# A block-streamed transformer kernel: order of the work ahead of the first cross attention's block loop

## The chip, the cores and the metric

The kernel runs on one NeuronCore of one Trainium2 chip. The metric is the device time of one execution in microseconds (us); the lower the better. The engines are named as in the profile: PE is the matrix engine (PEld its weight loads), DVE the vector engine, ACT the scalar engine, POOL the general one, and SP the engine that here only issues DMAs. Each runs its own instructions in order, and they wait for one another by semaphores.

## The reference, cut to what matters

Six layers act on x (512 tokens of 512 values): two cross attentions to a context of 8192 rows, two self attentions and two mixtures of experts. The change is in the first cross attention (L0x), which alone normalises queries and keys by head:

```python
q = (x @ Wq.T + bq).reshape(b, s1, h, d)          # x is layer-normed; h = 16 heads, d = 32
kv = (y @ Wkv.T + bkv).reshape(b, s2, 2, h, d)
k, v = kv[:, :, 0], kv[:, :, 1]
q = _ln(q, qn_w, qn_b) * scale                    # _ln: (t - mean) * rsqrt(var + 1e-6) * w + b, over d
k = _ln(k, kn_w, kn_b)
attn = jnp.einsum('bihd,bjhd->bhij', q, k)
attn = jnp.where(padding_mask[:, None, None, :], attn, -jnp.inf)
p = jax.nn.softmax(attn, axis=-1)
out = jnp.einsum('bhij,bjhd->bhid', p, v).reshape(b, s1, c) @ Wo.T + bo
```

## The kernel before, in words

The context is cut into blocks of 512 rows. A list of the blocks in which the mask lets anything through is made at run time; with these inputs the first cross attention has four. It makes two passes over them. The first (`row_maxima`) projects each block's keys and values, stores them in DRAM, and takes the maximum of every query's scores. The second (`weighted_values`) reads them back, takes exponentials and sums. The weights are centred by head first, so that a projected query or key has mean zero in every head, and only its variance has to be taken.

Keys and queries lie transposed, in four chunks of 128 features (four heads each). A block's 16 *quads* are the pairs (chunk c, 128 queries q), chunk by chunk. For a quad PE makes four heads' scores in two pairs of PSUM banks (`quad`, L676 for the scores, L687 adds the mask), and DVE takes a maximum over each pair (`maxima`, L1016, two of 1.2 us for a quad). There are three such pairs of banks: PE may start a half only when DVE is through with the half three before it. Behind each quad PE does two products that prepare the next block (`after_quad`, list `beside`): the key projections of block i + 1 in quads 0 to 7 (`project_keys`, L614, two chunks' worth in quads 0 to 3), then this block's value projections (`project_values`, L651). A product of 128 x 128 by 512 columns in fp32 shows as two matmul records. After quad 8 the variances of the next keys are taken (`variances`, L634), ACT makes roots, DVE inverts them after quads 9 and 10 (L980), and after quad 11 PE spreads them over the features (`spread`, L662) and DVE scales the keys (L987); ACT finishes them (`finish_keys`, L819). ACT also reads each projected chunk out of PSUM (`keys`: a square, L807, and the keys, L808), and in the first blocks counts masked entries of another mask for a later layer (`count`, L796) from four 1 MB loads that SP issues (L566). In the last block there are no next keys: quads 0 to 4 have no product behind them, and the value projections follow from quad 5 on.

Ahead of the loop there is a serial part that does the same for block 0's keys and for the queries. On PE: key projections, `variances(0)`, queries of chunks 0 and 1 (`all_queries`, L625), the spread of the keys (L760), `query_variances(0)` (L748), queries of chunks 2 and 3, `query_variances(2)`, and `query_spread` for both halves (L754). A *query half* is two chunks. ACT squares and reads the projected queries (`squared_query`, L836 and L837), takes roots (`query_roots`, L842), and at the end finishes keys and queries (L819, L846). DVE scales the keys (L1081), inverts a half's roots (`invert_query`, L1072), and then scales the four query chunks (`scale_query`, L1076), all after both inversions. PE enters the loop when all four are scaled.

SP's order: when block 0's keys are projected it loads the context of block 1 for the keys (CT, L516), when the queries are projected the context of block 0 for the values (XNT), then it stores each finished key chunk (L528), and then it enters its loop with the four mask loads.

Of the kernel before, what the change touches and what calls it, by code (L numbers as in the profile page):

```python
# [18 lines left out]
DC = D // P  # L19
# [407 lines left out]
def row_maxima(nc, m, L):  # L427
# [4 lines left out]
    dyn, norm = L.fixed is None, L.norm  # L432
# [28 lines left out]
    NK = DC + 1 if norm else DC  # L461
# [7 lines left out]
    def after_quad(k, todo, first=0):  # L469

        k, n = k - first, NS - first
        return todo[k * len(todo) // n:(k + 1) * len(todo) // n] if k >= 0 else []
# [5 lines left out]
        order.insert(SPREAD_AFTER + 1, "spread")  # L478
    NPAIR = 2 * len(order)
    PRE = 2 if norm else 0  # L480
    begun = L.keys_begun
    further = {sem: 16 for sem in values_stored}
    if begun:
# [24 lines left out]
    class Parts:  # L508
# [86 lines left out]
        def tensor(pe):  # L595
# [95 lines left out]
            def scores(i, ahead):  # L691
                for at, k in enumerate(order if ahead else range(NS)):
                    if k == "spread":
                        spread(i + 1, first_pair(i), at)
                        continue
                    quad(i, at, k)
                    if ahead and norm and k == VAR_AFTER:
                        variances(i + 1)
                    for kind, x, d in after_quad(k, beside) if ahead else after_quad(k, beside_last, 5 if dyn else 0):
                        if kind == "k":  # L700
                            project_keys(i + 1 if dyn else 0, x, d)
                        elif kind == "q":
                            project_queries(x, d)
                        else:
                            project_values(i, x, d, i + 2 if ahead else (i + 1 if dyn else 1))
# [6 lines left out]
            def all_queries(c):  # L712
                if norm:
                    pe.wait_ge(centred, 3 * c + 3)
                for d in range(DC):
                    project_queries(c, d)
# [26 lines left out]
            if norm:  # L743

                def query_variances(first):
                    pe.wait_ge(q_read, first + 2)
                    for c in (first, first + 1):
                        last = t.matmul(m.bank[6 + first // 2][rows(c), :], m.head_cols[:, 0:HD], m.SQ[:, c, :], start=True, stop=True)  # L748
                    last.then_inc(q_variance, 1)

                def query_spread(first):
                    pe.wait_ge(q_inverse, first // 2 + 1)
                    for c in (first, first + 1):
                        t.matmul(m.bank[2 + c], m.head_rows[rows(c), :], m.RSTDQ[rows(c), :], start=True, stop=True).then_inc(q_spread, 1)  # L754
# [7 lines left out]
                pe.wait_ge(k_read, NK + B)  # L762
                query_variances(0)
            all_queries(2)
            all_queries(3)
            if norm:
                query_variances(2)
                pe.wait_ge(scores_taken, PRE + B)
                query_spread(0)
                query_spread(2)  # L770
                pe.wait_ge(q_scaled, DC)
            if not begun:
                pe.wait_ge(wv_loaded, 16)
# [2 lines left out]
            def body(i):  # L776
                with pe.If(i + 1 < nb):
                    scores(i, True)
                with pe.If(i + 1 >= nb):
                    scores(i, False)  # L780

            active_loop(pe, nb, body)
# [3 lines left out]
        def scalar(act):  # L786
# [27 lines left out]
            def finish_keys(j, c, free):  # L814
                act.wait_ge(scores_taken, (B if free is None else spread_pair(free)) + c // 2 + 1)
                act.wait_ge(keys_stored[c], j * 16 + B)
                if free is not None:
                    act.wait_ge(scores_ready, chunk_scored(free, c))
                a.activation(m.KF[:, c, :], m.KW[:, c, :], ACT.Identity, bias=m.vec("kn_b")[:, 0:1],  # L819
                             scale=m.vec("kn_w")[:, 0:1]).then_inc(keys_final, 1)  # L820
# [12 lines left out]
            def squared_query(c):  # L833
                act.wait_ge(q_projected, c + 1)
                b = m.vec(L.bq)[:, c:c + 1]
                a.activation(m.SQ[:, c, :], m.bank[c % 2], ACT.Square, bias=b).then_inc(q_root, 1)  # L836
                a.activation(QF[:, c, :], m.bank[c % 2], ACT.Identity, bias=b).then_inc(q_read, 1)  # L837

            def query_roots(first):
                act.wait_ge(q_variance, first // 2 + 1)  # L840
                s = slice(HD * first, HD * (first + 2))
                a.activation(m.RSTDQ[s, :], m.bank[6 + first // 2][s, :], ACT.Sqrt, bias=m.EPS[s, :]).then_inc(q_root, 1)  # L842

            def finish_query(c):
                act.wait_ge(q_scaled, c + 1)
                a.activation(QF[:, c, :], QF[:, c, :], ACT.Identity, bias=m.vec("qn_b")[:, 0:1],  # L846
                             scale=m.vec("qn_w")[:, 0:1]).then_inc(query_ready, 1)
# [10 lines left out]
            if not begun:  # L858
                act.wait_ge(steps_done, 6)
                keys(0, 0)  # L860
                N.root(act)
                for c in range(1, DC - 1):
                    keys(0, c)
                N.copies(act)
                keys(0, DC - 1)
                key_roots(0)
                squared_query(0)
                squared_query(1)
                query_roots(0)
                squared_query(2)  # L870
                squared_query(3)
                query_roots(2)
                finish_keys(0, 0, None)
                finish_query(0)
                finish_keys(0, 1, None)
                finish_query(1)
                finish_keys(0, 2, None)
                finish_keys(0, 3, None)
                finish_query(2)
                finish_query(3)  # L880

            def masked(i):
# [5 lines left out]
            def body(i):  # L888
                if L.row_mask:
                    masked(i)  # L890

                def count_one(u):
                    if counting:
                        with act.If(i < NB // 4):
                            count(first_iterations(nc, i), u)

                with act.If(i + 1 < nb):
                    keys(i + 1, 0)
                    keys(i + 1, 1)
                    count_one(0)  # L900
                    keys(i + 1, 2)
                    count_one(1)
                    keys(i + 1, 3)
                    if norm:
                        key_roots(i + 1)
                    count_one(2)
                    values(i, 0)
                    values(i, 1)
                    if norm:
                        for c in range(DC - 1):  # L910
                            finish_keys(i + 1, c, i)
                    values(i, 2)
                    count_one(3)
                    values(i, 3)
                    if norm:
                        finish_keys(i + 1, DC - 1, i)
                with act.If(i + 1 >= nb):
                    for kb in range(KT_):
                        count_one(kb)
                        values(i, kb)  # L920
# [49 lines left out]
        def vector(dve):  # L970
# [94 lines left out]
            if norm:  # L1065
                for part in range(4):
                    invert(0, part)

                def invert_query(first):
                    dve.wait_ge(q_root, first + 2 + first // 2 + 1)  # L1070
                    s = m.RSTDQ[HD * first:HD * (first + 2), :]
                    v.reciprocal(s, s).then_inc(q_inverse, 1)  # L1072

                def scale_query(c):
                    dve.wait_ge(q_spread, c + 1)
                    v.tensor_tensor(QF[:, c, :], QF[:, c, :], m.bank[2 + c], ALU.mult).then_inc(q_scaled, 1)  # L1076

                for half in range(2):
                    dve.wait_ge(scores_ready, B + half + 1)
                    s = m.KW[:, 2 * half:2 * half + 2, :]  # L1080
                    v.tensor_tensor(s, s, m.pair[1 + half], ALU.mult).then_inc(scores_taken, 1)  # L1081
                invert_query(0)
                invert_query(2)
                for c in range(DC):
                    scale_query(c)
            else:
                dve.wait_ge(steps_done, 2)
                for c in range(DC):
                    dve.wait_ge(q_projected, c + 1)
                    v.scalar_tensor_tensor(QF[:, c, :], m.bank[c % 2], m.vec(L.bq)[:, c:c + 1],  # L1090
                                           m.RAROWS[:, :], ALU.add, ALU.mult).then_inc(q_read, 1)
# [1128 lines left out]
```

## Time and profile before

| | us |
|---|---|
| median of 3 runs | 1766.46 (1765.86 to 1768.48) |
| the profiled execution | 1768.05 |
| its span, first to last instruction | 1766.3 |
| PE busy, DVE busy, ACT busy in it | 1614.9, 1043.2, 510.7 |
| mean granted PE clock, share of full | 0.957 |

The span is what the rows below are cut from; starts are counted from its first instruction. The part ahead of the first cross attention's loop ends at 62.5 us, its four blocks begin at about 62.5, 122, 179 and 237 us, and its second pass begins at about 292 us. Busy shares say how long an engine worked, not whether anyone waited for it: that is read from the idle time before an instruction and from who ended it.

### The profile page before, as it was taken

Reading aid. Unit: us, or ns where it says so; the run is one execution under the profiler, and the core shown is the slowest. Engines: PE = TensorE matmul, PEld = TensorE weight load, DVE = VectorE, ACT = ScalarE, POOL = GpSimd, SP = SyncE. Lnnn points to the kernel's source line nnn. Section 1 sums busy time; section 2 is a strip of 40 time slices with the busy share of each in tenths; the row PEclk is TensorE's granted clock in tenths of the full one; section 3 lists DMA queues with packets and bytes.
Section 4 is the critical chain, followed back from the end, with each engine's and each line's share of the span. In section 5 each row is a group of like instructions: output and inputs, shape, how many; then the busy total and the mean of one; then the engine's idle time right before and its main releaser. Section 6 shows DMA issues by size and latency. Waiting matters only on the chain. (4 is left out here: it accounts for less than half of the span.)

```text
span 1766.3 us, 27736 instructions
## 1 busy us (share of the span) xinstructions
PE 1614.9 (91%) x9395; PEld 738.8 (42%) x9407; DVE 1043.2 (59%) x1683; ACT 510.7 (29%) x771; POOL 101.3 (6%) x82
## 2 busy tenths in 40 slices
PE   6899998999889889999999699998989789989997
PEld 3233333222333376666665233332222134467775
DVE  5677777999745541111112589997979845743223
ACT  2434325777313310000001111113657512200000
POOL 0100001000002010000001200000200000110001
PEclk9899979999989989999999799988999999989999
DMA  4333442211056966666661313220421021229996
GB/s 161 145 136 116 162 160 80 62 49 36 0 139 111 208 245 238 236 230 231 232 229 48 126 61 113 100 85 31 156 61 48 1 83 31 97 84 335 327 324 226
DMA packets 73577, 244.67 MB, mean 139 GB/s; under 512 B 7344, under 2 KB 20544, under 8 KB 53536
## 3 DMA queue, kind: packets, MB, share of 16 engines
q1 hardware_dynamic: 64896, 224.62, 38.6%
q10 hardware_dynamic: 6048, 10.69, 1.6%
q0 software_dynamic: 2560, 8.39, 1.4%
q8 instruction: 47, 0.77, 0.2%
q14 instruction: 26, 0.21, 0.0%
HBM read 218.24 MB, written 35.91 MB: 144 GB/s over the span
## 5 line engine op out<-in xcount | busy, mean ns | idle before, releaser
L1489 ACT ACTIVATE BIG<-banks 128x1024 f32<-128x1024 f32 (+5 forms) x320 | 282.1, 933 | 132.1 <-PE banks L1428 132.1
L1023 DVE CUSTOM_DVE_ANT_0 BIG<-banks,MASK,MX 128x512 bf16<-128x512 f32 (+5 forms) x384 | 229.1, 655 | 64.3 <-issue 36.8
L2010 PEld LDWEIGHTS banks<-KF,BIG 128*128 128x128 f32 x1792 | 226.9, 191 | 14.1 <-issue 14.1
L2010 PE MATMUL banks<-KF,BIG 128*128 128x160 f32 (+1 forms) x1792 | 229.4, 289 | 2.4 <-DVE KF L1737 2.0
L676 PE MATMUL banks<-KF,XN 32*128 32x512 f32 (+4 forms) x1280 | 200.6, 632 | 18.2 <-DVE MX L1023 9.2
L2038 PE MATMUL banks<-BIG,PB 128*128 128x512 f32 x448 | 202.9, 600 | 0.0
L1425 PE MATMUL banks<-XN,KF 32*128 32x512 f32 (+4 forms) x1280 | 173.7, 613 | 25.9 <-issue 6.9
L1539 DVE TENSOR_TENSOR PB<-PB,BIG 128x2048 f32<-128x2048 f32 (+5 forms) x78 | 166.6, 2136 | 25.5 <-ACT BIG L1489 23.9
L1016 DVE TENSOR_REDUCE MXW<-banks 128x2 f32<-128x1024 f32 x128 | 150.3, 1216 | 52.5 <-PE banks L687 51.5
L651 PE MATMUL banks<-WV,XNT 128*128 128x512 f32 x320 | 162.0, 627 | 0.0
L1391 PE MATMUL banks<-BIG,V 128*32 128x512 f32 (+4 forms) x1280 | 158.5, 566 | 3.7 <-ACT BIG L1489 2.8
L2038 PEld LDWEIGHTS banks<-BIG,PB 128*128 128x128 f32 x448 | 81.5, 190 | 113.1 <-issue 112.9
L676 PEld LDWEIGHTS banks<-KF,XN 32*128 32x128 f32 x1280 | 62.1, 192 | 156.8 <-DVE MX L1023 72.9
L614 PE MATMUL banks<-CT,WK 128*128 128x512 f32 x224 | 115.3, 643 | 4.6 <-DVE WK L419 4.6
L1425 PEld LDWEIGHTS banks<-XN,KF 32*128 32x128 f32 x1280 | 51.4, 187 | 141.6 <-ACT BIG L1489 107.5
L1927 ACT ACTIVATE PS<-banks 128x512 f32<-128x512 f32 x20 | 11.9, 597 | 335.3 <-PE banks L2038 300.8
L1806 DVE TENSOR_TENSOR PB<-V,banks 128x640 f32<-128x640 f32 x32 | 26.3, 821 | 118.6 <-ACT V L1913 114.4
L651 PEld LDWEIGHTS banks<-WV,XNT 128*128 128x128 f32 x320 | 54.6, 191 | 92.5 <-issue 82.9
L1539 DVE TENSOR_TENSOR PS<-PS,BIG 128x2048 f32<-128x2048 f32 (+5 forms) x39 | 82.9, 2126 | 5.7 <-ACT BIG L1489 4.3
L826 ACT ACTIVATE V<-banks 128x512 f32<-128x512 f32 x40 | 23.9, 597 | 210.0 <-PE banks L651 210.0
L1801 DVE TENSOR_SCALAR V<-banks 128x512 f32<-128x512 f32 x24 | 16.6, 691 | 114.8 <-PE banks L2010 112.5
L1539 DVE TENSOR_TENSOR BIG<-BIG 128x2048 f32<-128x2048 f32 (+5 forms) x39 | 80.4, 2062 | 3.8 <-ACT BIG L1489 3.1
(284 smaller groups left out, 1411.3 us busy)
## 6 DMA issues: line engine op xcount, KB each, us to landing
BIG<-in_L0f_w SPq DMA_DIRECT2D x64, 1024.0 KB, 4.8
BIG<-in_L1f_w SPq DMA_DIRECT2D x48, 1024.0 KB, 5.6
BIG<-in_mask_q SPq DMA_DIRECT2D x16, 1024.0 KB, 9.6
CT<-in_ctx SPq DMA_DIRECT2D x9, 1024.0 KB, 4.7
XNT<-in_ctx SPq DMA_DIRECT2D x8, 1024.0 KB, 5.8
k_saved<-KF SPq DMA_DIRECT2D x32, 256.0 KB, 2.6
v_saved<-V SPq DMA_DIRECT2D x24, 256.0 KB, 2.4
KF<-k_saved SPq DMA_DIRECT2D x24, 256.0 KB, 3.4
```

The lines of the kernel that those rows point to most:

```text
L614: last = t.matmul(bank, m.WK[:, d, x * P:(x + 1) * P], KSRC[:, d, :], start=d == 0, stop=d == DC - 1)
L651: last = t.matmul(value_bank(kb), VSRC[:, d, kb * P:(kb + 1) * P], m.WV[:, d, :], start=d == 0, stop=d == DC - 1)
L676: last = t.matmul(m.pair[(2 * at + half) % 3][:, e, k0:k1], QF[rows(g), c, q * P:(q + 1) * P], m.KF[rows(g), c, k0:k1], start=True, stop=n ...
L1016: v.tensor_reduce(m.MXW[:, H * q + h:H * q + h + 2], pair, AX.X, ALU.max).then_inc(scores_taken, 1)
L1023: last = v.tensor_tensor_reduce(m.JUNK[:, 2 * half + e, k0:k1], pair[:, e, k0:k1], bias, 1.0, mx, ALU.add, ALU.max, mx)
L1391: last = t.matmul(m.bank[6 + c % 2][rows(g), q0:q1], m.V[:, kt[k], HD * h:HD * h + HD], m.PE_[:, s % NP, g, q0:q1], start=k == 0, stop=k = ...
L1425: t.matmul(out(g), m.KF[rows(g), c, ks], m.QF[rows(g), c, q0:q1], start=not biases, stop=False)
L1489: a.activation(m.PE_[:, s % NP, 2 * half:2 * half + 2, q0:q1], m.pair[(2 * s + half) % 3][:, :, q0:q1], ACT.Exp).then_inc(exp_ready, 1)
L1539: v.tensor_tensor(dst, dst, m.PE_[:, s % NP, :, q0:q1], ALU.add).then_inc(sum_taken, 1)
L1806: v.tensor_tensor(out, ex, hidden[k % 2], ALU.mult).then_inc(hidden_copied, 1)
L2010: last = t.matmul(out, W1[k][:, d, f * P:(f + 1) * P], XE[:, d, :], start=d == 0, stop=d == DC - 1)
L2038: last = t.matmul(YB, HS[:, 4 * k + f, 0:P], W2[k][:, f, :], start=k + f == 0, stop=(k == NF - 1 and f == 3), skip_group_check=True)
```

## The change

The order of work ahead of the loop is rewritten for this one layer. PE spreads the first query half between the products of query chunk 3, and projects the first two key chunks of block 1 there; inside the loop quads 0 to 3 of block 0 no longer do so, which takes a test of the block's number in each of these quads in every block but the last. ACT finishes keys and the first query half between the squares, and reads the early key chunks ahead of the loop. DVE scales two query chunks behind each inversion.

```diff
--- before.py
+++ after.py
@@ -478,6 +478,8 @@
         order.insert(SPREAD_AFTER + 1, "spread")
     NPAIR = 2 * len(order)
     PRE = 2 if norm else 0
+    EARLY = 2 if norm else 0
+    EARLY_KEYS = [("k", x) for x in range(EARLY)]
     begun = L.keys_begun
     further = {sem: 16 for sem in values_stored}
     if begun:
@@ -696,7 +698,13 @@
                     quad(i, at, k)
                     if ahead and norm and k == VAR_AFTER:
                         variances(i + 1)
-                    for kind, x, d in after_quad(k, beside) if ahead else after_quad(k, beside_last, 5 if dyn else 0):
+                    todo = after_quad(k, beside) if ahead else after_quad(k, beside_last, 5 if dyn else 0)
+                    if ahead and todo[-1][:2] in EARLY_KEYS:
+                        with pe.If(i >= 1):
+                            for _, x, d in todo:
+                                project_keys(i + 1, x, d)
+                        continue
+                    for kind, x, d in todo:
                         if kind == "k":
                             project_keys(i + 1 if dyn else 0, x, d)
                         elif kind == "q":
@@ -762,12 +770,26 @@
                 pe.wait_ge(k_read, NK + B)
                 query_variances(0)
             all_queries(2)
-            all_queries(3)
-            if norm:
-                query_variances(2)
+            if not norm:
+                all_queries(3)
+            else:
+                pe.wait_ge(centred, 3 * DC)
+                project_queries(3, 0)
                 pe.wait_ge(scores_taken, PRE + B)
                 query_spread(0)
+                for d in range(1, DC):
+                    project_queries(3, d)
+
+                project_keys(1, 0, 0)
+                query_variances(2)
+                for d in range(1, DC):
+                    project_keys(1, 0, d)
+                pe.wait_ge(q_root, DC + 2)
+                project_keys(1, 1, 0)
+                project_keys(1, 1, 1)
                 query_spread(2)
+                project_keys(1, 1, 2)
+                project_keys(1, 1, 3)
                 pe.wait_ge(q_scaled, DC)
             if not begun:
                 pe.wait_ge(wv_loaded, 16)
@@ -777,6 +799,9 @@
                 with pe.If(i + 1 < nb):
                     scores(i, True)
                 with pe.If(i + 1 >= nb):
+                    if EARLY:
+                        with pe.If(i < 1):
+                            pe.wait_ge(k_read, NK + EARLY + B)
                     scores(i, False)
 
             active_loop(pe, nb, body)
@@ -867,16 +892,18 @@
                 squared_query(0)
                 squared_query(1)
                 query_roots(0)
+                finish_keys(0, 0, None)
+                finish_keys(0, 1, None)
+                finish_keys(0, 2, None)
                 squared_query(2)
+                finish_keys(0, 3, None)
+                finish_query(0)
+                finish_query(1)
                 squared_query(3)
                 query_roots(2)
-                finish_keys(0, 0, None)
-                finish_query(0)
-                finish_keys(0, 1, None)
-                finish_query(1)
-                finish_keys(0, 2, None)
-                finish_keys(0, 3, None)
+                keys(1, 0)
                 finish_query(2)
+                keys(1, 1)
                 finish_query(3)
 
             def masked(i):
@@ -895,8 +922,13 @@
                             count(first_iterations(nc, i), u)
 
                 with act.If(i + 1 < nb):
-                    keys(i + 1, 0)
-                    keys(i + 1, 1)
+                    if EARLY:
+                        with act.If(i >= 1):
+                            keys(i + 1, 0)
+                            keys(i + 1, 1)
+                    else:
+                        keys(i + 1, 0)
+                        keys(i + 1, 1)
                     count_one(0)
                     keys(i + 1, 2)
                     count_one(1)
@@ -1080,9 +1112,11 @@
                     s = m.KW[:, 2 * half:2 * half + 2, :]
                     v.tensor_tensor(s, s, m.pair[1 + half], ALU.mult).then_inc(scores_taken, 1)
                 invert_query(0)
+                scale_query(0)
+                scale_query(1)
                 invert_query(2)
-                for c in range(DC):
-                    scale_query(c)
+                scale_query(2)
+                scale_query(3)
             else:
                 dve.wait_ge(steps_done, 2)
                 for c in range(DC):
```

## Rows read from the trace of the kernel before

**Rows 1.** The page, busy us, share of the span and instructions of each engine:

```profile
PE 1614.9 (91%) x9395; PEld 738.8 (42%) x9407; DVE 1043.2 (59%) x1683; ACT 510.7 (29%) x771; POOL 101.3 (6%) x82
```

**Rows 2.** Timeline of PE, 52 to 63 us: start, us, operation [idle before <-releaser]:

```profile
52.69 1.05 PE L748 MATMUL banks<-BIG,CON 128*32 128x512 f32 x4 [1.36 <-ACT XN L837]
53.67 1.13 PE L754 MATMUL banks<-BIG,CON 32*128 32x512 f32 x4
57.91 2.08 PE L754 MATMUL banks<-BIG,CON 32*128 32x512 f32 x4 [3.11 <-DVE BIG L1072]
62.53 2.09 PE L676 MATMUL banks<-KF,XN 32*128 32x512 f32 x8 [2.55 <-ACT KF L819]
```

**Rows 3.** Timeline of the other engines, 33 to 61 us:

```profile
33.44 0.35 SPq L516 DMA_DIRECT2D CT<-in_ctx  x1
...
45.14 3.34 DVE L1072 RECIPROCAL BIG<-BIG 64x512 f32<-64x512 f32 x1
...
53.79 0.68 ACT L842 ACTIVATE BIG<-banks,EPS 64x512 f32<-64x512 f32 x1 [1.15 <-PE banks L748]
...
54.50 3.35 DVE L1072 RECIPROCAL BIG<-BIG 64x512 f32<-64x512 f32 x1 [6.02 <-ACT BIG L842]
...
60.01 1.29 DVE L1076 TENSOR_TENSOR XN<-XN,banks 128x512 f32<-128x512 f32 x2 [0.85 <-PE banks L754]
```

**Rows 4.** Stretches: us, busy of PE, PEld, DVE, ACT, POOL, granted clock, DMA, GB/s:

```profile
57.40:62.50 5.10, 2.08 (x4) 0.50 (x4) 3.48 (x6) 3.90 (x6) 2.77 (x2) 0.51 0.14 54
62.50:67.70 5.20, 5.17 (x16) 1.86 (x16) 2.35 (x2) 1.15 (x2) 0.00 (x0) 0.50 0.87 273
...
118.90:122.30 3.40, 1.85 (x8) 0.70 (x10) 2.18 (x3) 1.30 (x2) 0.00 (x0) 1.00 0.08 29
...
235.00:238.30 3.30, 1.76 (x14) 0.71 (x16) 1.26 (x4) 1.16 (x2) 0.00 (x0) 1.00 0.37 94
238.30:258.50 20.20, 19.32 (x66) 6.15 (x66) 13.94 (x12) 2.93 (x8) 0.00 (x0) 0.50 0.68 270
1163.40:1175.00 11.60, 11.45 (x34) 4.03 (x32) 11.60 (x35) 0.00 (x0) 0.00 (x0) 0.50 0.42 155
```

**Rows 5.** Timeline of the first block's first quads, 64 to 82 us:

```profile
64.98 3.32 PE L614 MATMUL banks<-CT,WK 128*128 128x512 f32 x4
65.07 2.35 DVE L1016 TENSOR_REDUCE MXW<-banks 128x2 f32<-128x1024 f32 x2 [3.31 <-PE banks L687]
...
68.23 1.14 PE L676 MATMUL banks<-KF,XN 32*128 32x512 f32 x8
...
69.61 2.36 DVE L1016 TENSOR_REDUCE MXW<-banks 128x2 f32<-128x1024 f32 x2 [2.19 <-PE banks L687]
...
71.43 1.14 PE L676 MATMUL banks<-KF,XN 32*128 32x512 f32 x8
...
72.82 2.36 DVE L1016 TENSOR_REDUCE MXW<-banks 128x2 f32<-128x1024 f32 x2 [0.85 <-PE banks L687]
...
81.04 1.14 PE L676 MATMUL banks<-KF,XN 32*128 32x512 f32 x8
```

**Rows 6.** The page, DMA issues: count, KB each, median us to landing:

```profile
CT<-in_ctx SPq DMA_DIRECT2D x9, 1024.0 KB, 4.7
```

**Rows 7.** Timeline of SP's DMAs behind the stores of block 0's keys:

```profile
63.64 2.56 SPq L566 DMA_DIRECT2D BIG<-in_mask_q  x4
```

**Rows 8.** Timeline of DVE, bare quads of the last block, 238 to 244 us:

```profile
238.11 2.36 DVE L1016 TENSOR_REDUCE MXW<-banks 128x2 f32<-128x1024 f32 x2 [0.49 <-PE banks L687]
241.53 2.36 DVE L1016 TENSOR_REDUCE MXW<-banks 128x2 f32<-128x1024 f32 x2 [1.06 <-PE banks L687]
```

**Rows 9.** Timeline of PE, first scores of the second and the last block:

```profile
121.94 1.14 PE L676 MATMUL banks<-KF,XN 32*128 32x512 f32 x8 [1.55 <-ACT KF L819]
...
235.35 1.14 PE L676 MATMUL banks<-KF,XN 32*128 32x512 f32 x8 [0.52 <-DVE MXW L1016]
```

## The prediction

> **What bounds the kernel now.** I read the page's busy table first: PE is busy 91% of the span, DVE 59% [rows 1]. A share over 1766 us doesn't say what one stage is worth, so I went to the stretch that the change touches, 33 to 122 us, and asked who waits for whom. Ahead of the first scores PE has two long waits: 3.11 us for the inversion of the second query half and 2.55 us up to the first scores [rows 2] (that wait is put down to a key chunk; by the timeline the last scaling of the queries ends at 60.01 + 1.29 = 61.30, and the first scores start at 62.53, so it is the scaling plus 1.23 us of loop entry) [rows 2, 3]. The chain there is serial: query chunk 3 projected, squared, its variance (52.69), root (53.79), inversion (54.50, 3.35 us), spread (57.91), scaling (60.01), first scores (62.53) [rows 2, 3]. PE does 3.21 us of work between 53 and 62 us and is granted half its clock from 57.4 on [rows 2, 4].
>
> In the first block a quad (the scores of one chunk for 128 queries, with its two maxima on DVE) starts at 62.53, 68.23 and then every 3.20 us up to 81.04: three identical steps of 3.20 lie between 71.43 and 81.04, and one before them [rows 5]. The first took 5.70 us, at half clock: its key projections alone took 3.32 us [rows 4, 5]. In the 3.20 us steps DVE works 2.36 and is idle 0.85, waiting for PE [rows 5]: PE is the bound, DVE would be the next at 2.36.
>
> **The change, part by part.** *The serial part.* PE now puts the spread of queries 0 and 1 behind the first quarter of chunk 3. Its input is inverted by 48.5 (it starts at 45.14 and takes 3.34) [rows 3], when PE is just there, so it doesn't stall; but it pushes the end of chunk 3 by its own length, about 0.9 of the 1.13 us that four such matmuls take with the drain of the last [rows 2]. So the chain to the second inversion starts 0.9 later: variance 53.6, root 54.7, inversion 55.4 to 58.75. The spread behind it took 2.08 us at half clock and takes 1.13 at full [rows 2]: scaling starts at 58.75 + 0.06 + 1.13 = 59.95 instead of 60.01. First scores at 62.47: 0.06 earlier. Bounds: if the moved spread costs nothing, 0.9 earlier; if PE is at half clock again, 0.9 later. Ending the first half early on DVE and ACT gains nothing by itself, as the second half was last before and still is.
>
> *The projections put into the hole.* Eight key projections, 16 matmul records of 0.43 us at full clock (4 of them fill 1.91 of a quad's 3.20), are 6.9 us. One product stands in the wait for the squares, three and two between the second variance and the second spread (54.6 to 58.9, 4.3 us against the 3.35 us inversion plus the root), two after it, 59.9 to 61.6. All end before 62.47, and DVE's scaling and the loop entry cover the last two. Their input was requested at 33.44 [rows 3]; the nine such loads land 4.7 us after their issue in the median [rows 6]. If the cover were gone the cost would be those last 1.7 us. On ACT the reading of key chunk 0 falls into the wait for the scaling, that of chunk 1 (1.3 us) delays query chunk 3 to about 63.5; it is wanted only in quad 12.
>
> *The queues.* SP loads the value context 0.9 us later (it waits for chunk 3), not wanted before quad 8. ACT finishes keys 0 to 2 ahead of the squares of query chunk 2, so SP stores them at once and the four mask loads of 1 MB, issued from 63.64 on behind the stores [rows 7], go out at about 56. They feed ACT's counting, which in ACT's order stands before key chunk 2, and are there earlier than before. POOL's memsets start 0.9 later and are used in the second pass only. Two projected chunks less in quads 0 to 3 also let SP ask for the next context sooner.
>
> *Quads 0 to 3 of the first block.* They lose their 1.91 us of projections each. What is late next is DVE, 2.36 per quad. The trace doesn't show such a quad at full clock, so I bound it: from below by two maxima back to back, 2.35 us; from above by the bare quads of the last block, which come every 3.42 us (238.11 to 241.53) [rows 8], but at half clock (granted 0.50 from 238.3 to 258.5) [rows 4]. There DVE's idle 1.06 us is PE's path from a freed bank to finished scores: 1.18 + 1.06 = 2.24 at half clock, 1.12 to 1.2 at full, which DVE's 1.18 covers. I take 2.40.
>
> *The sum.* Start 62.47; first maximum 1.38 later (69.61 less 68.23) at 63.85; four quads of 2.40 bring quad 4's first maximum to 73.45; the scores of quad 5 start 1.82 later (71.43 less 69.61), at 75.27. Before it was 81.04 [rows 5]. Gain 5.8 us, 2.5 of it the half clock of quad 0, 3.2 the four shorter quads. From quad 4 on all is as before, relative to it: PE is the bound at 3.20, and the block end is set by the same chain.
>
> *The new branches.* In blocks 1 and 2 each of quads 0 to 3 has a test (8 in all), in block 0 a jump over nothing but two products. In block 0 DVE is the bound and hides it. In the others PE's sequencer waits for a freed bank in every quad while its array still has projections to do: nothing. From the other side, a whole block change with its several branches left 0.52 us of idle PE [rows 9], so 8 tests cost at most 4.2. I take 0: one test is small against 1.9 us of queued projections. The Trainium skill, "Advanced Engine Details and Errata", section Control Flow Timing, gives about 108 ns for a compare-and-branch; uncovered, that would be an estimated 0.9 us. No row here shows it alone. The last block's new wait holds only when there is one block; here there are four.
>
> The profiled execution took 1768.05 (span 1766.3, 1.75 around it) and would come to 1762.2; the median of the runs is 1.6 below it: 1766.46 − 5.8 = 1760.7.
>
> **The rivals.** *Half clock throughout (the other side).* Bare quads leave PE about a third idle and use 32 of 128 rows per matmul. Both stretches of such quads in this trace, 238.3 to 258.5 and 1163.4 to 1175, were granted 0.50 and never came back while they lasted, though PE counts as busy 19.32 of 20.2 us and 11.45 of 11.6 there [rows 4]. Each time the clock had fallen at a block change: 1.76 us of work in 3.3 ahead of 238.3 [rows 4]. For it: the entry to the first block is such a place. Against: 1.85 of 3.4 us ahead of 122.3 kept full clock [rows 4], and now PE works from 54.6 to 61.6 almost without a gap. Price: start 62.47, first maximum 2.54 later (65.07 less 62.53), four quads of 3.42, quad 5 another 3.16 later (68.23 less 65.07): 81.85, 0.8 slower, 1767.3; if quad 5 is also still at half clock, 2.5 more, 1769.8. It decides when the clock falls in quad 0. The Trainium skill, "TensorE: Matmul & The Clock Gate", section "A second HAM failure mode: psum-queue depth-cycling", says that small idles between groups of matmuls while cycling through banks make the clock go back and forth: by that rule this rival or the next holds; the rows at 238 and 1163 agree, and no row shows bare quads that begin at full clock.
>
> *The clock falls midway, in quad 2 or so.* Two quads at 3.42, and quad 4's projections at half clock: about 3.3 to 4.5 of the 5.8 are given back, 1764.6.
>
> *The time is given back.* Block 0 gets sooner to something that doesn't move: mask, context or the key chain. All of these start earlier or with the block, so little speaks for it: 1766.5.
>
> *A further clock outcome.* Everything after is shifted. If the last block's bare quads keep full clock, five quads gain 1.0 each: 1755.7. Against: nothing at that boundary changes but the phase.
>
> **How the numbers follow.** Forecast (full clock through quads 0 to 3) 0.52, own range 1759 to 1763; falling midway 0.16; half clock throughout 0.14; given back 0.09; further gain 0.09. The range 1756 to 1767.8 leaves out most of the 1769.8 branch and a part of the last case, under 2 in 10. 0.2% (3.5 us, what a measurement of this kernel can tell from no change) puts the line at 1762.9 and 1770.0: faster 0.49 of the forecast, 0.04 of midway, 0.09 of the last, 0.62; slower 0.08, for which the half-clock case needs a branch cost of the kind bounded above on top; the rest, 0.30, is no change.
>
> **What would show it.** Right: L614's early products between 53 and 62 us; the first scores at 62.5 within 0.5; granted clock 1.00 from 54 to 80; four pairs of maxima 2.35 to 2.45 apart, then 3.20; quad 5 near 75.3; block 1's first scores near 116.1 instead of 121.94 [rows 9]. Wrong: maxima 3.42 apart, or a clock of 0.50 between 60 and 75; first scores after 63.5; quads of blocks 1 and 2 longer than 3.20 with idle PE; a gain at 81 that is gone at 292.

## The result: 0.24% slower, and the profile after

The changed kernel takes 1770.9 us in the median of 15 runs (1768.52 to 1776.37), the kernel before 1766.46 on the same chip. The ratio is 1.0024, with a 95% interval of 1.0013 to 1.0036: slower by some 4 us, where 1760.7 had been forecast. The profiled execution took 1774.38 (span 1772.6), that of before 1768.05.

The order of PE ahead of the loop became what was intended. Timeline of PE in the changed kernel (start, us, operation, idle before):

```profile
52.67 1.05 PE L756 MATMUL banks<-BIG,CON 128*32 128x512 f32 x4 [0.50 <-ACT XN L862]
53.66 4.56 PE L616 MATMUL banks<-CT,WK 128*128 128x512 f32 x10
58.14 1.13 PE L762 MATMUL banks<-BIG,CON 32*128 32x512 f32 x4
59.20 1.98 PE L616 MATMUL banks<-CT,WK 128*128 128x512 f32 x4
61.73 1.14 PE L678 MATMUL banks<-KF,XN 32*128 32x512 f32 x8 [0.55 <-issue]
...
75.19 3.78 PE L616 MATMUL banks<-CT,WK 128*128 128x512 f32 x4
78.90 1.14 PE L678 MATMUL banks<-KF,XN 32*128 32x512 f32 x8
```

The holes of 3.11 and 2.55 us [rows 2] are gone, and quad 5 starts its scores at 78.90 instead of 81.04 [rows 5]. DVE in the same kernel, and two stretches (busy of PE, PEld, DVE, ACT, POOL, granted clock, DMA share, GB/s):

```profile
63.11 7.30 DVE L1048 TENSOR_REDUCE MXW<-banks 128x2 f32<-128x1024 f32 x6 [2.07 <-PE banks L689]
71.48 2.35 DVE L1048 TENSOR_REDUCE MXW<-banks 128x2 f32<-128x1024 f32 x2 [1.07 <-PE banks L689]
74.90 2.35 DVE L1048 TENSOR_REDUCE MXW<-banks 128x2 f32<-128x1024 f32 x2 [1.07 <-PE banks L689]
80.29 2.35 DVE L1048 TENSOR_REDUCE MXW<-banks 128x2 f32<-128x1024 f32 x2 [3.03 <-PE banks L689]
```

```profile
62.50:68.50 6.00, 5.33 (x34) 1.79 (x28) 5.15 (x5) 3.68 (x10) 0.00 (x0) 1.00 1.01 419
68.60:78.80 10.20, 9.98 (x28) 2.95 (x24) 6.52 (x6) 0.00 (x0) 0.00 (x0) 0.50 0.19 76
```

Quads 0 to 2 ran at full clock, their six maxima without a gap. Then the clock was granted at 0.50 (1.2 of 2.4 GHz) from 68.6 to 78.8: quads 3 and 4 are 3.42 apart, just like the bare quads of the last block [rows 8], and quad 4's projections take 3.78 instead of 1.98. So this block was only 2.1 us ahead at quad 5. Blocks 1 and 2 nearly held that: matched instruction by instruction, the lead goes from 2.14 us at 82 us to 1.97 at 235.

After the first pass it turned. By PE's instructions the changed kernel was 0.83 us behind from 300 us on, 3.0 behind at 660, 4.3 from 1000 on, 9.1 at 1390, and 6.3 behind at the end. One of the places, PE in the second cross attention's second pass, in code that the change doesn't touch:

```profile
1368.80 1.86 PE L1459 MATMUL banks<-XN,KF 32*128 32x512 f32 x8 [3.35 <-issue]
```

"<-issue" says that nothing in the profile kept PE waiting. In the kernel before, the same line has such a gap of 3.57 us at 1318, but none here. The waits of PE that end so, by the line that waited (us in total, times, longest; L1425 of before is L1459 here), first before, then after:

```profile
PE banks L1425 <- issue: 6.9, 2, 3.6
PE banks L1215 <- issue: 6.9, 2, 5.0
```

```profile
PE banks L1459 <- issue: 10.3, 3, 3.9
PE banks L678 <- issue: 3.3, 3, 1.9
```

What moves 16 KB around these gaps is seen in DMA queue 8 ("instruction"): of before between 1395 and 1406 us, where PE idled 4.99 us ahead of L1215, it carried three packets and no other queue anything:

```profile
DMA packets 3, 0.05 MB, mean 4 GB/s; under 512 B 0, under 2 KB 0, under 8 KB 0
q8 instruction: 3, 0.05, 1.7%
```

By the queue's name it is the engines' code that is fetched there; which engine's, the view doesn't say. The change made PE's code longer: counted in the built programs, PE has 9877 instructions before and 9922 after, so all PE code behind the first pass stands 45 later. (In the compiled code most unconditional jumps of that count are gone, and it has 9835 and 9876, branch labels left out, which no trace shows executed. There the later code stands 41 later.) ACT's code grew too, from 850 to 858 in the compiled code. The prediction had no term for any of that. The Trainium skill, "Runtime: NRT & Kernel Launch", section Instruction fetch mechanics, says that code comes in 16 KiB blocks of 256 instructions, and that a taken branch out of the blocks at hand waits for a fetch; 0.05 MB in three packets agrees with the first, the 4.99 us beside them with the second.

### The profile page after: what moved, and what is told of

It reads as the page before. It is cut to its first block and busy times, and to the rows that moved or that the text cites. A ratio compares the mean times of both kernels' runs of the same rounds, so it can differ in the third digit from the quotient of the medians.

```text
span 1772.6 us, 27766 instructions
## 1 busy us (share of the span) xinstructions
PE 1628.5 (92%) x9406; PEld 743.2 (42%) x9407; DVE 1043.2 (59%) x1683; ACT 510.9 (29%) x771; POOL 99.9 (6%) x82
## 5 line engine op out<-in xcount | busy, mean ns | idle before, releaser
L678 PE MATMUL banks<-KF,XN 32*128 32x512 f32 (+4 forms) x1280 | 206.3, 636 | 17.0 <-DVE MX L1055 9.0
L1459 PE MATMUL banks<-XN,KF 32*128 32x512 f32 (+4 forms) x1280 | 175.3, 618 | 28.9 <-issue 10.3
L1425 PE MATMUL banks<-BIG,V 128*32 128x512 f32 (+4 forms) x1280 | 160.8, 571 | 5.2 <-ACT BIG L1523 2.8
L1459 PEld LDWEIGHTS banks<-XN,KF 32*128 32x128 f32 x1280 | 51.6, 188 | 145.8 <-ACT BIG L1523 107.4
L851 ACT ACTIVATE V<-banks 128x512 f32<-128x512 f32 x40 | 23.9, 597 | 211.1 <-PE banks L653 211.1
```

Source lines behind the costliest of these rows:

```text
L678: last = t.matmul(m.pair[(2 * at + half) % 3][:, e, k0:k1], QF[rows(g), c, q * P:(q + 1) * P], m.KF[rows(g), c, k0:k1], start=True, stop=n ...
L1425: last = t.matmul(m.bank[6 + c % 2][rows(g), q0:q1], m.V[:, kt[k], HD * h:HD * h + HD], m.PE_[:, s % NP, g, q0:q1], start=k == 0, stop=k = ...
L1459: t.matmul(out(g), m.KF[rows(g), c, ks], m.QF[rows(g), c, q0:q1], start=not biases, stop=False)
```

## The experiments

All were run in five rounds beside the kernel before; ratios are to it, with the 95% interval. The theory of *place*: the loss comes from where the later PE code stands, not from the new order. The rival, *work*: the new order itself, its branches or its transfers cost it. "Place" below is how many instructions later than in the kernel before the PE code behind the first pass stands, modulo 256, as the runs were planned by the built programs; "compiled" is the same in the compiled code, without labels, with a minus where it falls short of a multiple of 256.

| run | what it is | place | compiled | ratio | 95% |
|---|---|---|---|---|---|
| (the change) | | 45 | 41 | 1.0024 | 1.0013 to 1.0036 |
| e1 | before, moved | 45 | 44 | 1.0045 | 1.0029 to 1.0062 |
| e7 | before, moved, moved back later | 45, then 0 | 44, then -2 | 1.0016 | 0.9999 to 1.0034 |
| e6 | before, moved | 128 | 127 | 0.9932 | 0.9909 to 0.9954 |
| e2 | the change | 0 (256) | -5 | 0.9996 | 0.9980 to 1.0012 |
| e9 | the change | 128 | 123 | 0.9921 | 0.9890 to 0.9953 |
| e4 | order alone | 0 | 0 | 1.0000 | 0.9983 to 1.0018 |
| e3 | one product a quad | 0 (256) | -17 | 0.9956 | 0.9938 to 0.9974 |
| e5 | four useless products | 0 (256) | -9 | 0.9937 | 0.9914 to 0.9960 |
| e8 | e3, last block too | 0 (256) | -17 | 0.9907 | 0.9882 to 0.9932 |
| e10 | e8 | 128 | 111 | 0.9863 | 0.9834 to 0.9892 |

**The place alone.** The moving is done by instructions that are never executed:

```diff
             active_loop(pe, nb, body)
+            if norm:
+                with pe.If(nb < 1):              # never: nb is 4
+                    for _ in range(10):
+                        t.matmul(m.bank[6], m.WK[:, 0, 0:P], m.CT[:, 0, :], start=True, stop=True)
...
             return nb
```

> The kernel before with 45 PE instructions that are never executed behind the first cross attention's first pass (a branch jumps over them), so that all later PE code stands where it stands in the changed kernel; the first pass itself is as before. Theory A (the loss is where the code stands: PE fetches its code in 16 KB pieces and loops cross other borders): the later layers lose what they lost in the changed kernel, about 6 us (2.1 gained by 82 us, 4.4 lost at the end), ratio to before 1.002 to 1.004, and the trace has the 3.35 us PE stall without a releaser in the second pass of the second cross attention, near 1364 us. Theory B (the loss is chance of the clock after the shift in time): ratio 1.000 within 0.001, no such stall.

Measured: 1780.21 us against 1772.49 in the same batch, 1.0045. Adding 45 instructions that never run costs what the whole change cost or more, and ACT's code is here as it was before. This trace has PE's longest gap of this kind, in the same pass as the changed kernel's:

```profile
1377.93 1.23 PE L1433 MATMUL banks<-XN,KF 32*128 32x512 f32 x4 [6.93 <-issue]
```

```diff
 changed kernel, behind its first pass
+                    for _ in range(52):   # in the same never-taken branch: 211 instructions
+                        t.matmul(...)
```

> The changed kernel with 211 PE instructions that are never executed at the same place: later PE code is shifted by 256 instructions (16 KB) in all, so its borders fall as in the kernel before. Theory A: the gain of the first pass is left, about 2 us: 1764 to 1766, ratio 0.998 to 1.000, no 3.35 us stall near 1364 us. Theory B: as the changed kernel, ratio about 1.0024.

Measured: 1771.83, 0.9996. With 45 + 211 = 256 the later code is at its old place modulo 16 KB (within five instructions in the compiled code), and the loss is gone, though ACT's code is as long as in the changed kernel. But so is most of the forecast gain: this trace too falls to half clock, at 69.1 for 10.2 us, and its quad 5 starts at 79.16.

```diff
 kernel before: e6 has 31 products and one small one in the branch (128 instructions)
 kernel before: e7 has e1's 45, and 211 more behind the second cross attention's first pass
+            if L.row_mask:
+                with pe.If(nb < 1):
+                    for _ in range(52):
+                        t.matmul(...)
```

> As e1 with 128 PE instructions that are never executed in place of 45: half a 16 KB piece. Theory A: the later layers change by some other amount, of either sign, between 0.997 and 1.006, with stalls at other loops than e1's; the first pass is the same as before. Rival (any dead code costs the same, by its jump or its fetch): ratio 1.0045 as e1.

> e1's 45 PE instructions at the same place, and 211 more never executed behind the first pass of the second cross attention: the two layers between them stand as in e1, all from the second pass of the second cross attention on as before (256 in all). Theory A: the stalls near 1364 to 1374 us of e1 are gone, those near 586 and 600 us stay; of e1's 7.7 us (1.0045) some 4 to 5 us go: ratio 1.001 to 1.0025. Rival: the loss isn't tied to where each loop's code stands: 1.0045 as e1.

Measured: e6 1758.48 against 1770.33, 0.9932, the largest single effect of any place, and a gain beyond the 0.997 that had been expected as its limit. e7 1.0016: undoing the move behind the second cross attention's first pass takes away e1's gap of 6.93 us, as the theory has it, and brings back the kernel before's near 1405 us (4.98 us), which e1 lacks. It leaves those at 588 and 601 us (1.07 and 1.23 us), but that shows little, since the kernel before idles 0.94 and 1.89 us there. The interval just reaches 1, and the profiled execution also lost some 5 us at 1606 us, where PE waited 5.17 us for a DMA. The waits by issue of e6:

```profile
PE banks L1433 <- issue: 3.0, 1, 3.0
PE banks L1223 <- issue: 1.7, 1, 1.7
```

Both were 6.9 us in the kernel before; what is left of L1433 is a gap near 1218 us, and the one near 1318 is gone. The code fetches of the whole run fall from 47 to 44 packets, in e9 and e10 too. That the gap costs twice is seen where it goes: in the kernel before the clock was granted at 0.50 for 6.8 us from 1317.0 on and again from 1402.3 on, right at the gaps of 3.57 and 4.99 us; e6 has no half clock at the first and 3.4 us of it, from 1390.7 on, at the second. Its trace gains 5.6 us over the first and 4.0 over the second.

> The changed kernel with 83 never-executed PE instructions behind its first pass, so that the PE code behind that point stands 128 instructions later than in the kernel before (the changed kernel alone stands 45 later; the other two places tried are 256, where it was 0.9996 of before, and 45, 1.0024). Theory 'place': the place works by itself, whatever is changed in the first pass, and what the change itself is worth at one place is what it is at another. In the place of 128 the kernel before was 0.9932; the change alone was 0.9996 at 256 and 1.0024/1.0045 = 0.998 at 45, so 0.991 to 0.994 here, some 1753 to 1757 where before takes 1768; no stall of PE over 1 us at 585 to 600 and at 1313 us. Rival 'luck of the phase': what the place gave before the change was chance of that one program; then anything from 0.995 to 1.003, as with the changed kernel so far.

Measured: 1756.26 against 1769.88, 0.9921. The place works on the changed kernel as on the one before. Between e9 and e2 only the count of dead instructions differs (83, 211), and 0.75% with it. PE comes through the point at which the kernel before and e2 stall; first e2, then e9 (where, against the expectation, one gap of 1.19 us is left at 596 us):

```profile
1317.83 1.60 PE L1467 MATMUL banks<-XN,KF 32*128 32x512 f32 x8 [3.54 <-issue]
```

```profile
1311.79 1.14 PE L1467 MATMUL banks<-XN,KF 32*128 32x512 f32 x8 [1.11 <-ACT BIG L1531]
1314.47 1.14 PE L1467 MATMUL banks<-XN,KF 32*128 32x512 f32 x8 [0.33 <-ACT BIG L1531]
```

All twelve traces, put in order by the compiled place, suggest what "place" decides. The gap of 3.5 to 3.9 us near 1318 us of the kernel before is there at -5, -2, 0, 41 and 44 and nowhere else. The one near 1405 us, with 5.0 to 6.7 us, is there from -17 to 0, is not there at 41 and 44, and has 1.75 us from 111 on. The ones near 1364 us (3.35 and 6.93 us) are there at 41 and 44 alone. This order was seen afterwards, in one execution for each kernel, and holds without the labels only (with them the first gap would be there at 0 to 9 and at 46 and 53, but not at 13 and 21), and another gap of some 3 us, near 1218 us, doesn't follow it: e1, e2 and e9 lack it, their neighbours have it. So the place very likely decides the largest gaps, but not every one.

**The order alone.** EARLY = 0: the new order of spreads and scalings stays, the eight key projections go back into quads 0 to 3.

```diff
-    EARLY = 2 if norm else 0
+    EARLY = 0
...
-                project_keys(1, 0, 0)
                 query_variances(2)
...
```

> Only the new order of the serial part (spread of the first query half between the products of chunk 3, scaling and finishing by halves); no key chunk of block 1 is projected early and the loop is as before. PE has exactly as many instructions as before, so no border moves. Theory: first scores within 0.5 us of 62.5 less the start shift, quad 0 at half clock again (5.7 us): ratio 1.000 within 0.001. Rival (the half-wise order itself gains or costs): first scores earlier or later by 1 us or more.

Measured: 1772.56, 1.0000. Its PE code is as long as before (9877). The serial chain became longer, as the rival had it: first scores came at 62.79 although this trace was 1.0 us ahead at 30 us, so 1.3 us later than before net of that; the time doesn't show it. The clock falls even earlier (half clock for 13.7 us from 55.5 on), with PE's hole ahead of the second spread at 4.17 us instead of 3.11:

```profile
58.16 2.08 PE L762 MATMUL banks<-BIG,CON 32*128 32x512 f32 x4 [4.17 <-DVE BIG L1094]
```

**The clock.** Two ways to keep PE loaded in quads 0 to 3. e5 leaves the change as it is and adds a product that nobody reads; e3 spreads the eight remaining key projections of chunks 2 and 3 over quads 0 to 7, one each.

```diff
 e5, block 0, behind each of quads 0 to 3
                         with pe.If(i >= 1):
                             for _, x, d in todo:
                                 project_keys(i + 1, x, d)
+                        with pe.If(i < 1):
+                            if k == 0:
+                                pe.wait_ge(k_read, NK + 1 + B)
+                            t.matmul(m.bank[6], m.WK[:, 0, 0:P], m.KW[:, 0, :], start=True, stop=True)
 e3, block 0, behind each of quads 0 to 7
+                        with pe.If(i < 1):
+                            project_keys(i + 1, EARLY + k // DC, k % DC)
```

> As e2 (the changed kernel, its later PE code shifted by 256 instructions in all), with one product that nothing reads behind each of quads 0 to 3 of block 0: four useless products of 0.86 us of PE. Theory (the clock falls because bare quads give PE too little, not because of the order or the tests): the clock stays 1.00 from 54 to 95 us, quads 0 to 3 come every 2.5 us as in e3, quad 4's projections take 1.98 instead of 3.78, and the first pass ends 3.5 to 4.5 us earlier than e2's: ratio to before 0.997 to 0.9985 although there is more work. Rival (time, not load: the clock would fall there whatever PE does, since it is some 11 us after the gap at the loop's entry): falls near 69 again, and e5 is the same as e2 or up to 3 us slower.

> As e2, but in block 0 the eight products of key chunks 2 and 3 stand one behind each of quads 0 to 7, in place of none in quads 0 to 3 and two in quads 4 to 7. Theory of the clock (bare quads let it fall): with one product in each quad the granted clock stays 1.00 from 54 to 95 us, quads 0 to 7 come every 2.4 us, and quad 8 starts near 62.0 + 8 x 2.4 = 81.5 against 91.7 in the changed kernel and 93.85 less the shift of 1.3 in the kernel before: 7 to 9 us less than e2's first pass, ratio to before 0.994 to 0.996. Rival (something else than the clock stretched the quads, such as PE's path from a freed bank to finished scores, or the tests in the loop): the quads stay at 3.2 to 3.4 us or fall at half clock anyway, and e3 is within 2 us of e2.

Measured: e5 1760.07 against 1770.33, 0.9937, more than the 0.997 to 0.9985 expected; e3 1764.72 against 1772.49, 0.9956, as expected. DVE and the two stretches in e5:

```profile
63.47 4.83 DVE L1060 TENSOR_REDUCE MXW<-banks 128x2 f32<-128x1024 f32 x4 [2.06 <-PE banks L689]
68.46 4.83 DVE L1060 TENSOR_REDUCE MXW<-banks 128x2 f32<-128x1024 f32 x4 [0.17 <-PE banks L689]
73.45 2.36 DVE L1060 TENSOR_REDUCE MXW<-banks 128x2 f32<-128x1024 f32 x2 [0.17 <-PE banks L689]
76.78 2.36 DVE L1060 TENSOR_REDUCE MXW<-banks 128x2 f32<-128x1024 f32 x2 [0.97 <-PE banks L689]
```

```profile
62.50:68.50 6.00, 6.00 (x41) 2.08 (x33) 4.75 (x5) 4.04 (x10) 0.00 (x0) 1.00 1.00 416
68.60:78.80 10.20, 10.20 (x52) 3.79 (x56) 8.94 (x8) 0.09 (x1) 0.00 (x0) 1.00 0.23 92
```

PE is busy in all of both stretches, the clock stays at 1.00, the quads come every 2.50 us, and quad 5 starts its scores here:

```profile
75.40 1.14 PE L678 MATMUL banks<-KF,XN 32*128 32x512 f32 x8
```

Four products of about 1 us that compute nothing make this block 3.5 us shorter up to here than the changed kernel. That is all the clock of these quads is worth: against e2, whose trace ends 12 us behind e5's, the lead is 3.8 us behind the first block, and another 4.5 come around the gap near 1318 us, which e5 lacks. The Trainium skill, "TensorE: Matmul & The Clock Gate", section "A second HAM failure mode: psum-queue depth-cycling", names small idles between groups of matmuls as what makes the clock go back and forth; 5.33 us busy of 6.00 ahead of the fall and 6.00 of 6.00 where it didn't fall agree. But a product differs from the scores in more than that it fills the idles: it uses 128 rows and not 32. In the changed kernel PE was busy for 9.98 of the 10.20 us at half clock, most of them with bare quads, and full clock came back only at 78.8, after quad 4's two products. Whether the idles or the kind of work let the clock fall is not shown: e3 and e5 change both.

e3 keeps the clock with useful work: eight quads of 2.50 instead of four of 2.40 and four of 3.20.

```profile
63.64 4.83 DVE L1058 TENSOR_REDUCE MXW<-banks 128x2 f32<-128x1024 f32 x4 [2.06 <-PE banks L689]
68.63 4.83 DVE L1058 TENSOR_REDUCE MXW<-banks 128x2 f32<-128x1024 f32 x4 [0.17 <-PE banks L689]
73.63 4.83 DVE L1058 TENSOR_REDUCE MXW<-banks 128x2 f32<-128x1024 f32 x4 [0.17 <-PE banks L689]
78.62 4.83 DVE L1058 TENSOR_REDUCE MXW<-banks 128x2 f32<-128x1024 f32 x4 [0.17 <-PE banks L689]
```

Its trace is 8.3 us ahead of the kernel before from 97 us on, 6.5 more than e2. Of that 1.2 go in the last block and 1.8 at 300 us, as in e2; another 3.7 go between 575 and 625 of the kernel before's time, where this trace has gaps by issue of 1.06, 2.38 and 1.35 us. So e5's lead over e3 in the whole time isn't the first block's: there e3 is 2.6 us ahead of e5. It comes from later places. Both e3 and e5 lack the gap that e2 has near 1318 us, although all three were planned for one place; in the compiled code they stand at -17, -9 and -5, which the order above would account for.

**The last block too, and the best place.** e8 is e3 with the last block's value projections from quad 3 instead of 5, so that fewer bare quads stand there; e10 is e8 at place 128.

```diff
-                    todo = after_quad(k, beside) if ahead else after_quad(k, beside_last, 5 if dyn else 0)
+                    todo = after_quad(k, beside) if ahead else after_quad(k, beside_last, (3 if norm else 5) if dyn else 0)
```

> As e3, and in the last block the value projections begin behind quad 3 instead of quad 5: three bare quads at half clock instead of five. Theory of the clock: bare quads cost 3.42 us each at half clock, and the clock comes back once products follow; the block is 2 to 3 us shorter, ratio to before 0.9935 to 0.995. Rival (the values' context, loaded at the block's start, comes too late for quad 3, or the clock comes back no sooner): same as e3, 0.9956.

> The kernel of the run with one product a quad and the last block's value projections from quad 3 on (0.9907 at the place of 256), with 25 instead of 153 never-executed PE instructions, so that the later PE code stands 128 later than in the kernel before. Theory 'place': both add, 0.9907 x 0.9932 = 0.984, about 1740 where before takes 1768. Rival 'luck of the phase': the same 0.990 to 0.992 as at 256.

Measured: e8 1755.83 against 1770.33, 0.9907, a larger gain than the 0.9935 expected at best; e10 1744.42 against 1769.88, 0.9863. What the last block gives in e8 shows in its half-clock stretch, from 240 to 255 us (first before, then e8):

```profile
240.00:255.00 15.00, 14.15 (x56) 4.63 (x50) 9.89 (x9) 2.93 (x8) 0.00 (x0) 0.50 0.85 344
```

```profile
240.00:255.00 15.00, 15.00 (x64) 4.74 (x60) 11.21 (x10) 4.32 (x12) 0.00 (x0) 0.78 0.30 125
```

Against the kernel before, e8's lead grows from 8.25 us ahead of the last block to 10.56 behind it. At the end its trace is 7.6 us ahead of e3's, 3.7 of them since the last block; the rest comes in later layers, whose code both have alike and at one place, and isn't explained. e10 is the fastest version here, 1.4% faster than the kernel before and 1.5% than the changed one (1744.42 / 1770.9, in different batches). The product of e6 and e8 would be 0.984; 0.9863 has it inside its interval, but a third of the way back to e8's 0.9907. e8 already lacked the gap near 1318, so only the one near 1405 was left to win: between 1390 and 1410 us e10's lead grows by 5.3 us, e8's shrinks by 1.5.

## Why the prediction was wrong, step by step

*The serial part: right in kind, 0.5 too hopeful.* First scores were forecast at 62.47 and came at 61.73, but that they came early is luck: 1.27 us of lead were there before the first changed instruction. PE's first 24 matmul records took 12.20 us instead of 13.42, with full clock on record from 17.4 us on instead of 19.9; e2, e5 and e9 had 0.9 to 1.0 us of the same, and e1 and e6, which change nothing there, 0.24 and 0.76. Net of it the first scores came 0.47 us later than before, not 0.06 earlier. The moved spread pushed the chain by 1.25 us (variance at 52.67, and 52.69 less 1.27 is 51.42), where 0.9 stood in the sum. The second spread waits behind the key product in front of it (58.14, where the inversion had ended at 57.84), and the entry of the loop shows 0.55 us by issue.

*Four bare quads of 2.40: 2.43 to 2.47 where the clock was full* (six maxima in 7.30 us, and 2.47 between PE's starts at 64.39 and 66.86; 2.50 with one product more in e5). Right in size, also that DVE is late next.

*"Full clock through quads 0 to 3": the step that failed in the first block.* It held for three quads. The rival "falls midway" is what happened, with 3.3 to 4.5 us of loss forecast and 3.5 measured between quad 5 of the changed kernel (78.90) and of e5 (75.40). What had been said against a fall at the entry, that PE works there almost without a gap, held (53.66 to 61.18), and the clock fell all the same, behind three bare quads. It had been given 0.16, the forecast 0.52. e5 nearly has the forecast's number for quad 5 (75.40, forecast 75.27) at full clock, with 0.9 us of lead from the start. e2 and e9 fell within 0.5 us of the same point as the changed kernel, so this is not chance: three traces of three.

*From quad 4 on as before: right for the first pass.* Quads 3.20 apart in blocks 1 and 2, and a lead that changes by 0.17 us in 153.

*The new branches at 0: right but for 0.17 us.* The lead falls by 0.08 or 0.09 us in each of blocks 1 and 2, in e2, e5 and e9 alike, and by 0.01 at most in e1, e6 and e7, which have no tests: some 0.02 us a test. *The queues: right.* The four mask loads went out at 56.01, forecast about 56, instead of 63.64 [rows 7], and quads 0 to 2 ran beside them at DVE's pace.

*The missing term: the place of the later code.* This carried the sign. With the change's order and the old place modulo 256 the kernel is at 0.9996 (e2); with the old order and the new place at 1.0045 (e1). The prediction priced the instructions that run and not the 45 that push others. The change by itself is therefore worth 0 to 0.2%, with ratios that are uncertain by 0.2 to 0.4%: e2 over before 0.9996, the change over e1 1.0024/1.0045 = 0.998, e9 over e6 0.9921/0.9932 = 0.999. The first block's 0.9 us net of the luck at the start (2.14 less 1.27) fits these.

In the one pair of traces, the 8.3 us from 2.0 ahead at 235 us to 6.3 behind at the end are made up so: 1.1 in the last block (half clock for 23.9 us instead of 20.5), 1.7 at 290 to 300 (half clock for 10.2 us instead of 6.8), 2.2 at 575 to 660, 1.2 at 975, 4.8 at 1350 to 1390, 2.3 given back at 1405, and half a us given back behind that. The 2.3 show that a place isn't bad or good as a whole: the gap of 4.99 us ahead of L1215 in the kernel before is 1.79 us at 1410.96 in the changed one. The first two are no matter of place 45: e2, e3, e6, e7 and e9 have them too (1.1 to 1.2 and 1.7 to 1.8), e1 only the second (2.1), and e4 and e5 neither. They are a phase of the clock that several versions happen to fall into, and I can't say what decides it. Of the other 5.5 us the gaps by issue and the clock's falls at them are the larger part, but one execution doesn't split them cleanly.

## What to carry to other kernels

Before a change of a few us is judged by its time, look whether it moves code: run the kernel before with as many never-executed instructions, and the change with its length padded to a whole 16 KB, counted in the compiled code; here the place alone spans 0.9932 to 1.0045, more than the edit. Where DVE sets the pace, don't empty PE: take out only as much as leaves it just busy, and spread the rest evenly; here the clock fell behind three bare quads and took 3.5 us back.

## What the runs showed of the hardware

- 128 never-executed PE instructions made an unchanged kernel 0.68% faster (0.46 to 0.91), 45 made it 0.45% slower (0.29 to 0.62).
- Single gaps of PE that ended by "issue" took up to 6.93 us at untouched code (e1), and in the kernel before half clock for 6.8 us followed on two of them, at 1317.0 and 1402.3.
- PE at 5.33 of 6.00 us busy with bare quads held full clock for 6 us and then fell; at 6.00 of 6.00 with one product more in each quad it didn't fall. Which of the two, the time filled or the product's 128 rows, keeps it isn't shown.
- Eight run-time tests in PE's quads (four in each of two blocks) cost 0.17 us together.
- With the later code -5, -2, 0, 41 or 44 instructions from its old place modulo 256, PE idled 3.5 to 3.9 us near 1318 us; at -17, -9, 111, 123 and 127 it didn't.
